# First state-space scan relaid in state-by-feature partitions, its rows through DRAM; B read from PSUM in both passes

## The reference

```python
x1 = ssm(layernorm(h)) + h        # first scan: the state-space layer L0_attn
#   hid  = silu(x @ w1 + b1) for A, B, C (384 wide each) and d (192 wide)
#   A = -|hid_A @ A_w2 + A_b2|, Bv, Cv the same way (16 states per token); delta = sigmoid(hid_d @ d_w2)
#   state[f,n] = (delta[f]*state[f,n] + (1-delta[f])*x[f]*B[n]*dt[f]) * exp(A[n]*dt[f])
#   y[f] = sum_n state[f,n]*C[n] + x[f]*D_param[f]
x2 = moe_top2(layernorm(x1)) + x1 # 8 experts, 768 wide, exact gelu
x3 = up(ssm_f(down) + ssm_b(down)) + x2   # two Mamba directions, forward and backward, 192 features x 16 states
out = mixture of 8 linear experts(layernorm(x3)) + x3
```

## Time and profile before

| | us |
|---|---|
| median of 3 runs (1111.74 to 1113.39) | 1113.3 |
| profiled execution, its own time | 1113.84 |
| span of its trace | 1112.1 |
| up to the first scan's input ready | 0 to 65.8 |
| first pass, four scans and the last output | 65.8 to 372.6 |
| last group's routing, tables | to 399.4 |
| experts | to 571.0 |
| second pass: first preparation | to 617.4 |
| second pass: eight directions | to 1042 |
| tail | to 1112.1 |

### The profile page before, as it was taken

How to read it: one execution, slowest core, us unless ns; L and a number is a source line. 1 busy time by engine, 2 the same in 40 slices (tenths; PEclk the granted TensorE clock), 3 DMA queues, 4 the chain that set the end, 5 groups by cost and what they waited for, 6 DMA issues and landing times.

```text
span 1112.1 us, 11242 instructions
## 1 busy us (share of the span) xinstructions
PE 763.2 (69%) x3558; PEld 547.1 (49%) x3558; DVE 715.0 (64%) x967; ACT 433.3 (39%) x847; POOL 484.2 (44%) x300
## 2 busy tenths in 40 slices
PE   3777776877755329999836458566777687775755
PEld 2443444544423229999815245444554555553523
DVE  3089899789799231211111688899878987999420
ACT  1336535434421103333314446464726371644120
POOL 0038654746755430101120275574467546646503
PEclk9686888887765559999958559688979788966957
DMA  9600000000000038999610866666575647567102
GB/s 352 265 33 1 9 33 1 26 1 1 26 1 1 27 94 267 302 293 294 214 26 18 199 169 168 165 175 170 136 201 155 163 130 215 144 174 179 31 7 70
DMA packets 63470, 137.22 MB, mean 123 GB/s; under 512 B 10276, under 2 KB 26416, under 8 KB 62656
## 3 DMA queue, kind: packets, MB, share of 16 engines
q1 hardware_dynamic: 58784, 130.09, 41.0%
q0 software_dynamic: 4496, 6.55, 2.0%
q10 hardware_dynamic: 144, 0.02, 0.0%
HBM read 118.45 MB, written 18.14 MB: 123 GB/s over the span
## 4 chain that ended last, share of the span: by engine, by line
DVE 32%; PE 32%; issue 11%; POOL 9%; DMA 8%; ACT 5%; SPq 2%; DVEq 0%; POOLq 0%; ACTq 0%
PE PS L1527 31%; DVE ST L1175 6%; DVE ST L1206 5%; POOL PR L711 4%; DVE BB L1172 4%; DMA BB<-rows_d 3%; DVE BB L1168 2%; DVE BB L1192 2%; POOL slots_d L674 2%; DMA xp<-outs_d,slot_u 1%; POOL xp L697 1%; DMA WXR<-ex_r 1%; DMA CR<-c 1%; POOL q_TM L645 1%; DVE PR L1184 1%
## 5 line engine op out<-in xcount | busy, mean ns | idle before, releaser
L1527 PE MATMUL PS<-PR,CM 128*128 128x152 f32 (+1 forms) x512 | 152.4, 448 | 97.1 <-POOL PR L711 97.1
L1206 DVE TENSOR_TENSOR_SCAN ST<-dA,BB 128x608 f32<-128x608 f32 x96 | 165.4, 1726 | 12.4 <-POOL PR L711 12.3
L1527 PEld LDWEIGHTS PS<-PR,CM 128*128 128x128 f32 x512 | 105.1, 242 | 133.5 <-POOL PR L711 112.8
L863 ACT ACTIVATE dA<-dA,negA 128x304 f32<-128x304 f32 x192 | 93.9, 539 | 154.8 <-DMA BB<-rows_d 154.4
L711 POOL TENSOR_TENSOR PR<-ST,p_V 128x608 f32<-128x608 f32 x48 | 107.9, 2259 | 93.1 <-DVE ST L1206 90.4
L711 POOL TENSOR_TENSOR PR<-ST,q_V 128x608 f32<-128x608 f32 x48 | 84.5, 1763 | 130.5 <-DVE ST L1206 121.4
L652 POOL TENSOR_TENSOR aP<-dA,p_DL 128x912 f32<-128x912 f32 x32 | 72.9, 2281 | 138.5 <-DVE q_UP L1233 77.0
L1527 PE MATMUL PS<-p_S,SEL 128*64 128x152 bf16 (+1 forms) x576 | 82.8, 317 | 73.0 <-DVE PR L1184 41.1
L1527 PEld LDWEIGHTS PS<-p_S,SEL 128*64 128x64 bf16 (+1 forms) x576 | 30.2, 120 | 131.5 <-issue 48.2
L960 ACT ACTIVATE HID<-PS,WX 128x128 f32<-128x128 f32 x162 | 47.8, 365 | 109.5 <-PE PS L1527 109.5
L1175 DVE TENSOR_TENSOR_SCAN ST<-aP,BB 128x912 f32<-128x912 f32 x32 | 89.2, 2787 | 1.1
(11 more groups left out here) (337 smaller groups left out, 1626.1 us busy)
## 6 DMA issues: line engine op xcount, KB each, us to landing
dA<-rows_d SPq DMA_DIRECT2D x96, 304.0 KB, 3.7
BB<-rows_d SPq DMA_DIRECT2D x96, 304.0 KB, 4.4
WX<-ex_m SPq DMA_DIRECT2D x27, 576.0 KB, 4.6
WX<-ex_m SPq DMA_DIRECT2D x27, 387.0 KB, 4.0
slots_d<-WXR SPq DMA_DIRECT2D x8, 960.0 KB, 28.2
WXR<-ex_r SPq DMA_DIRECT2D x27, 192.0 KB, 5.1
WX<-gates_d SPq DMA_DIRECT2D x4, 1216.0 KB, 6.3
CM<-c SPq DMA_DIRECT2D x1, 4430.0 KB, 20.3
```

The costliest lines, as they stand in the source:

```text
L863: last = nc.scalar.activation(dAq[:, slot, i, :], dAq[:, slot, i, :], ACT.Exp, scale=negA[:, j:j + 1])
L1206: nc.vector.tensor_tensor_scan(flat(STq[:, c % 2], back), flat(dAq[:, slot], back), flat(BBq[:, slot], back), 0.0, ALU.mult, ALU.add).then ...
L1527: return nc.tensor.matmul(out, lhsT, rhs, start=first, stop=last)
```

## The change

It has two parts. In the first pass the scan now uses the second pass's layout: 12 steps of 2 feature blocks, 128 x 608. `m2_w` holds the second-layer weights of A, B and C with columns repeated 8 times, so that three groups of three matmuls (`states`) give A, B and C already replicated over the features of a block; ACT takes |A + bias| to SBUF, adds B's bias in place in PSUM and copies C. Delta and w go to `rows_d` in DRAM (alternate halves for alternate groups) and come back through the ring. `p_decay` writes exp(-|A|*dt) into a ring of its own, EXPS = 3, which multiplies both delta (POOL, `decay_step`) and w*B (DVE). The product with C moves from DVE to POOL (`first_product`), the sum over states from POOL to PE (`first_sum`). The bf16 split, `SEL` and the spreading matmuls are gone. `first_scan_input` of group p moves from behind the end of scan s to step 7 of it, the output of m to step 0, the patches of the next group to PE's step 10, and the hidden layers run in larger lots on PE and ACT at steps 4, 5 and 6 over two banks, those of delta first; the scatter is at steps 9 to 11. In both passes B stays in PSUM (banks 1 and 2) and DVE multiplies from there; in the second pass ACT's copy of B is gone and the output norm uses the Y banks.

```diff
-            def scan_step(g, c):
-                dve.wait_ge(P.b_bc.sem, P.b_bc.after(g, c + 1))
-                nc.vector.tensor_tensor(BB[:, c % 2], P.WV[:, :].unsqueeze(1).broadcast_to([128, NC, PK]),
-                                        PS[:, B_BANK:B_BANK + NC, 0:PK], ALU.mult).then_inc(P.b_read.sem, 1)
...
+            def first_b_product(g, c):
+                slot = c % SLOTS
+                if c == 0:
+                    dve.wait_ge(b1_ready.sem, b1_ready.after(g, 1))
+                dve.wait_ge(P.landed[slot].sem, P.landed[slot].after(g, 32 * landings(0, c)))
+                nc.vector.tensor_tensor(BBq[:, slot], BBq[:, slot], PS[:, BW_BANK[g % 2], 0:T].unsqueeze(1).broadcast_to([128, QB, T]),
+                                        ALU.mult).then_inc(P.b_times_w.sem, 1)
+            def first_step(g, c):
+                if c == 0:
+                    first_b_product(g, 0)
+                if c + 1 < QSTEPS:
+                    first_b_product(g, c + 1)
...
+                nc.vector.tensor_tensor(BBq[:, slot], BBq[:, slot], EXq[:, c % EXPS], ALU.mult).then_inc(b_times_a.sem, 1)
+                dve.wait_ge(b_times_a.sem, b_times_a.after(g, c + 1))
+                dve.wait_ge(ap_ready.sem, ap_ready.after(g, c + 1))
+                if g or c >= 2:
+                    dve.wait_ge(P.product.sem, P.product.after(g, c - 1))
+                nc.vector.tensor_tensor_scan(flat(STq[:, c % 2], False), flat(dAq[:, slot], False),
+                                             flat(BBq[:, slot], False), 0.0, ALU.mult, ALU.add).then_inc(P.scanned.sem, 1)
...
             def b_product(g, k, c):
                 if c == 0:
-                    dve.wait_ge(bc_copied.sem, bc_copied.after(g, 2 * k + 1))
+                    dve.wait_ge(b_mm.sem, b_mm.after(g, k + 1))
                 dve.wait_ge(landed[slot].sem, landed[slot].after(g, 32 * landings(k, c)))
-                nc.vector.tensor_tensor(BBq[:, slot], BBq[:, slot], DIRS[k].Bw.unsqueeze(1).broadcast_to([128, QB, T]),
+                nc.vector.tensor_tensor(BBq[:, slot], BBq[:, slot], PS[:, BW_BANK[k], 0:T].unsqueeze(1).broadcast_to([128, QB, T]),
                                         ALU.mult).then_inc(b_times_w.sem, 1)
```

POOL's and ACT's part of a first-pass step, and PE's:

```diff
+            def decay_step(s, c):
+                slot = c % SLOTS
+                pool.wait_ge(P.landed[slot].sem, P.landed[slot].after(s, 32 * landings(0, c)))
+                pool.wait_ge(P.decay_ready.sem, P.decay_ready.after(s, c + 1))
+                nc.gpsimd.tensor_tensor(dAq[:, slot], dAq[:, slot], EXq[:, c % EXPS], ALU.mult).then_inc(ap_ready.sem, 1)
+            def first_product(s, c):
+                pool.wait_ge(P.scanned.sem, P.scanned.after(s, c + 1))
+                if s or c >= 2:
+                    pool.wait_ge(P.summed.sem, P.summed.after(s, c - 1))
+                nc.gpsimd.tensor_tensor(PRq[:, c % 2], STq[:, c % 2], CS[s % 2][:, :].unsqueeze(1).broadcast_to([128, QB, T]),
+                                        ALU.mult).then_inc(P.product.sem, 1)
...
+            def p_decay(g, c):
+                if g or c >= EXPS:
+                    act.wait_ge(b_times_a.sem, b_times_a.after(g, c - EXPS + 1))
+                    act.wait_ge(ap_ready.sem, ap_ready.after(g, c - EXPS + 1))
+                for i in range(QB):
+                    last = nc.scalar.activation(EXq[:, c % EXPS, i, :], AS[g % 2][:, :], ACT.Exp, scale=neg_dtq[:, j:j + 1])
...
+            def first_sum(g, c):
+                pe.wait_ge(P.product.sem, P.product.after(g, c + 1))
+                add_states(Y_BANK[g % 2], c).then_inc(P.summed.sem, 1)
```

More of the change, by code:

```diff
@@ L656, in first, with scatter @@
+            def scatter(m, t):
+                for k in range(2):
+                    pool.indirect_dma_start(slots_d[:, :], bass.IndirectOffsetOnAxis(slot_u[:, t, k:k + 1], 0),
+                                            XTOK[0:TW, t, :], None).then_inc(scattered.sem, 16)
             def first(s, p, m):
-                if s is not None:
-                    pool.wait_ge(P.w_ready.sem, P.w_ready.after(s, 1))
-                    decay_step(s, 0)
-                for c in range(STEPS):
+                for c in range(QSTEPS):
@@ L807, in hidden @@
             def hidden(g, first, last):
-                for j in range(first, last):
-                    act.wait_ge(hid_mm.sem, hid_mm.after(g, j + 1))
+                for i in range(first, last):
+                    j = HIDDEN_ORDER[i]
+                    act.wait_ge(hid_mm.sem, hid_mm.after(g, i + 1))
                     dst, rows = (HID[:, j, :], 128) if j < 10 else (HIDr, DR)
-                    nc.scalar.activation(dst, PS[0:rows, HIDDEN_BANKS[j], 0:T], ACT.Silu,
+                    nc.scalar.activation(dst, PS[0:rows, HIDDEN_BANKS[i % 2], 0:T], ACT.Silu,
                                          bias=cm("m1_b", j, j + 1, p=rows)).then_inc(hid_ready.sem, 1)
@@ new lines, in first @@
+                    if n == 4:
+                        if m is not None:
+                            logits(M, m, ROUTE_BANK, None)
+                        if p is not None:
+                            hidden(p, 0, 4)
+                    if n == 5 and p is not None:
+                        act.wait_ge(P.ln_x.sem, P.ln_x.after(p, 1))
+                        if s is not None:
+                            act.wait_ge(P.w_ready.sem, P.w_ready.after(s, 1))
+                        nc.scalar.activation(P.UP[:, 0:T], P.Xm[:, :], ACT.Copy)
+                        nc.scalar.activation(P.UP[0:DR, T:PK], P.Xr[:, 0:HALF], ACT.Copy)
+                        nc.scalar.activation(P.UP[DR:128, T:PK], P.Xr[:, HALF:T], ACT.Copy).then_inc(packed_x.sem, 1)
+                        hidden(p, 4, 8)
@@ L1756, in first @@
+                    if n == 8 and m is not None:
+                        pe.wait_ge(xtok_copied.sem, xtok_copied.after(m, 1))
+                        token_rows(m, (2,))
+                    if n == 10 and follows(p) is not None:
+                        patches(p + 1)
+                    if s is not None and n:
+                        first_sum(s, n - 1)
+                    if n == 2:
                         if p is not None:
-                            hidden(p, 6, 7)
-                    if s is not None and c + 1 < STEPS:
-                        spread_c(s, c + 1)
@@ L1791, in first @@
-                    if c == 7 and p is not None:
-                        for i, (name, first, count, bank) in enumerate((("m2_w0", 0, 6, 7), ("m2_w1", 6, 3, 4))):
-                            pe.wait_ge(hid_ready.sem, hid_ready.after(p, (8, 10)[i]))
-                            for j in range(count):
-                                last = mm(PS[:, bank, 0:T], cm(name, j * NBLK, (j + 1) * NBLK), HID[:, first + j, :], j == 0, j == count - 1)
-                            last.then_inc(P.set_mm.sem, 1)
-                            if i == 0:
-                                hidden(p, 9, 10)
-                                pe.wait_ge(P.set_copied.sem, P.set_copied.after(p, 1))
-                                hidden(p, 10, 11)
```

633 lines of the change are left out of this document (262 added, 371 removed).

## The result

The changed kernel takes **1079.9 us** (median of four runs, 1075.9 to 1081.7) beside 1113.2 (1111.7 to 1113.4): ratio 0.970, 95% interval 0.967 to 0.973, 33.4 us less. Forecast: 1073, 40 us less. The profiled execution took 1080.1, its span is 1078.3.

A forecast was written before the change was run, and what follows sets the result against it. Bound: turns between POOL and DVE operations with two SBUF inputs, more than DVE itself. 1113.84 - 22.4 (first pass) - 18 (second pass) = 1073.4, so 1073 us; forecast's own range 1058 to 1088, 8 in 10 from 1050 to 1105.

The forecast's parts named there:

- Turns as the resource: POOL and two-SBUF-input DVE operations take turns, PSUM-input ones do not; plain first-pass step of four turns: 4.84 us.
- The whole-record rival: Both passes: a turn lasts the whole record, step 5.17 us, second pass gains half or nothing; 1089 to 1107 us, chance 0.17.
- Second pass, -18: B's product leaves the turns, saving 0.45 us a step only where DVE waits for POOL: 18 us less.
- the two ends, 0 and 43: Limits of the second pass's gain: nothing, or 0.45 us in each of 96 steps, 43 us.
- rival 1: B in PSUM frees every second-pass step: 1048 us, anything down to 1058 counted; chance 0.13.
- Where it starts, 70.7: First group, no cover: w_ready at 56.8, DRAM rows 13.2, one more product 0.8; scan 0 at 70.7, 1.8 later than before.
- The groups: First pass: 66.4 us for the group with no m, 73.0 for each of two full ones, 65.7 for the last.
- +1.8: Last three steps of a group: two scatters each behind two POOL operations, 5.7 us for 4.84, together +1.8.
- +0.7: Next group's step 0: what the preceding scatters on POOL add there, 0.7 us.
- Hidden layers, 35.0 us from scan 3 to scan 8: First-pass steps to 8: gates wait for logits queued behind PE's layers; 35.0 us against 24.2 plain, +10.8.
- Rival 2: First pass: PE stays at 1.2 GHz and its sums hold POOL, 48 us more, 1121; chance 0.15 for 1108 and above.
- DRAM rows hidden: First-pass row reads, issued at scan c-4 and used two steps later, have 9.7 us against 4.4 of landing: no cost.

The follow-up runs named there:

- e1: Changed kernel with B back in SBUF for the second pass's products, copied there by ACT: 1099.0 us, ratio 0.9870.
- e2: Changed kernel with B written to SBUF by ACT and read there by the first pass's products: 1091.2 us, ratio 0.9824.
- e4: Changed kernel with scatters one each in the next group's steps 0 to 5, landing awaited in step 6: 1069.7 us, ratio 0.9606.
- e8: Changed kernel with only POOL's wait for the scatters' landing moved from the group's end to the next group's step 2: 1079.9 us, ratio 0.9703.
- e9: e8 plus a POOL wait for DVE's tokens before step 1's decay, in groups with tokens to write: 1077.6 us, ratio 0.9697.
- e3: Changed kernel with PE's state sums and logits' transposes ahead of the next group's hidden layers, steps 4 to 7: 1077.9 us, ratio 0.9705.
- e6: e3 plus ACT's exponentials ring 4 deep, filled 3 ahead, and delta's sigmoid ahead of hidden layers 4 to 10: 1069.4 us, ratio 0.9602.
- e7: e6 combined with e4's scatters, one each in the next group's steps 0 to 5: 1054.4 us, ratio 0.9464.
- e10: e7 with scatters in steps 0 to 4, two in step 3, and POOL's landing word in step 5: 1051.5 us, ratio 0.9463.

## Why the prediction was nearly right

The profiled execution took 1080.1 us, the forecast for one like it was 1073.4. By stages it missed by +7.1 in the first pass and +3.3 in the experts, and was ahead by 3.0 in the second pass and 0.9 in the rest. That the total came so near is luck in part: inside the first pass, too, an early start hides 3.0 of 10.1 us.

- **Turns as the resource: right.** Plain steps 4.81 (forecast 4.84), products with B of 0.77 in both passes; e1 and e2 put B back and paid 19 and 14 us. The whole-record rival (5.17) is out.
- **Second pass, -18: right.** -21.0 in the profiled execution, 19.1 by e1. The kernels with B in PSUM had 390 to 396 us from first to last scan, the two without 412. Since this pass is the same code in all but e1, those 390 to 396 us are also its scatter. Of the two ends, 0 and 43, neither was near; rival 1 (-43) is out. One sign did not come: the scans' mean is 1.67 us (before 1.73), not below 1.6. The time inside records went from B's products, 89.9 to 74.0 us, more than from the scans, 165.4 to 160.2. The forecast counted the products of one direction only; this row of the kernel before, of the other, has 40.0 - 48 x 0.76 = 3.5 us of waiting more, some 3 steps:
```profile
L1192 DVE TENSOR_TENSOR BB<-BB,p_R 128x608 f32<-128x608 f32 x48 | 40.0, 841 | 0.1
```
- **Where it starts, 70.7: too late by 3.0.** Here is the start after:
```profile
50.31 0.38 ACT L929 ACTIVATE p_DL<-PS,WX 128x152 f32<-128x152 f32 x1
53.27 0.33 SPq L466 DMA_DIRECT2D rows_d<-p_DL  x1
63.06 0.79 DVE L1152 TENSOR_TENSOR BB<-BB,PS 128x608 f32<-128x608 f32 x1 [9.81 <-DMA BB<-rows_d]
67.72 1.42 DVE L1169 TENSOR_TENSOR_SCAN ST<-dA,BB 128x608 f32<-128x608 f32 x1
```
  The rows were ready at 53.3, not 56.8; from there to the first scan 14.4 (forecast 13.9). The mis-sized term is the eleven layers' time: priced from the earlier trace rows with four slow layers (9.6 us), it had two, and nine fast. The two, with the first eight matmuls, at a granted clock of 0.50:
```profile
32.28:36.49 4.21, 4.21 (x8) 2.86 (x9) 0.00 (x0) 0.88 (x2) 0.00 (x0) 0.50 1.02 427
```
  In the kernels whose start was not edited the first scan began at 65.6 to 68.2.
- **The groups.** From scan 0 to scan 0: 64.2, 74.3 and 78.2 us (forecast 66.4, 73.0, 73.0), and from the last scan 0 to the output 72.9 (67.1 by the forecast's terms). The sum is +10.1; with the start's -3.0 it is the 7.1 us by which the last output, 357.3, missed 350.2.
- **The step that failed: "the last three steps have slots and, on POOL, two scatters each ... +1.8, and +0.7 in the next step 0".** It priced POOL's time alone, 2.5 us. The runs show 5.9 us at a boundary (e4), since POOL's lateness lets its next operation in ahead of the waiting scan. It is the +0.7 that failed: from scan 8 to the next scan 0 the two boundaries took 20.0 and 19.3 us against 18.0 in e4, 2.0 and 1.2 for the +1.8; from scan 0 to scan 1 10.5 and 10.1 against 7.0 and 5.1, 3.5 and 5.0 for the +0.7. The wait for the store's landing was not in the forecast at all, and its price is no simple term: without it POOL shuts DVE out instead (e8), and with that mended 2.2 us of the step are left to gain (10.5 to 8.3, e9).
- **Hidden layers, 35.0 us from scan 3 to scan 8: right in kind, 2.8 short.** 37.9 and 37.7 us in the full groups between starts (36.8 and 36.5 between ends of scans). The reason given, that the gates wait for logits queued behind layers on PE, was half of it: e3 took that queue away and gained nothing. At the start and in the first group ACT's order is the bound (e6: 7.2 and 3.7 us). For the full groups this is argued from waits that moved to ACT each time (e3, e6); no run shortened them. The forecast did have ACT's loads and packs in its chain, but named PE.
- **Rival 2 (PE's sums hold POOL): its sign came, its cost not.** POOL waited for sums 6.8, 6.9 and 5.9 us a group, over the 5 that the forecast had set as its refutation, at a clock of 0.74 to 0.85. e3 removed these waits for nothing. The threshold was badly chosen: a wait proves no cost where another engine is as late.
- **DRAM rows hidden: right.** No scan of a later group waited for a landing; the waits for rows are the two before the first scan.

Left open: what the scatters cost in their new place. From scan 3 to scan 8 the last group takes 30.7 us in e6, 35.7 in e7 and 32.3 in e10; why e7's 5.0 are not fewer was not tried apart from the word in step 6.

## What to carry to other kernels

Where VectorE and GpSimd work on SBUF side by side, price turns, not engines. Leave one of VectorE's inputs in PSUM where turns set the step (it gained nothing where VectorE waited for something else, e2); and when one engine becomes late, add to its lateness the next operation that it will have ready, for it goes first. A wait that vanishes from one engine is only a gain if no other engine stood behind the same work: e3 took away 28 us of waits and gained no time in the groups.

## What the runs showed of the hardware

- A hand-over of a turn comes 0.1 us before the record's end (a plain step is 4.81 us, by whole records it would be 5.17), and POOL's product starts 0.15 us behind the start of the DVE operation that follows the scan (94.41 and 94.56). So a DVE operation put between the two costs 0.46 us of its 0.76 (e2).
- A ready engine keeps its turn: POOL ran 3 operations, 4.3 us, past a waiting DVE copy of 0.17 us, and in the next group past a waiting product (e8). Adding a wait of 0.55 us to POOL made the step 4.1 us shorter (e9). A plain copy with one SBUF input takes part in this as well.
- The granted clock of TensorE fell from 0.84 to 0.74 between the first and third group of the first pass; plain steps, which wait for VectorE and GpSimd, lasted 4.81 us in both.
